# Which sorted edge keys of a segment are counted one by one, and which are first sorted out of a common rest: 76 counting blocks in place of 88

## The reference, cut to what matters

```python
src, dst = edge_index                       # drawn from 0 .. 32767, there are M = 8192 nodes
e     = leaky_relu(a_src[src] + a_dst[dst]) # 4 heads
ee    = exp(e - segment_max(e, dst)[dst])
alpha = ee / (segment_sum(ee, dst)[dst] + 1e-16)
agg   = segment_sum(h[src] * alpha, dst)    # for each node
w     = softmax of the 2 best of 4 scores(layernorm(agg))
out   = x + sum over experts e of w_e * (gelu(x @ W1[e] + b1[e]) @ W2[e] + b2[e])
```

## Time and profile before

| | |
|---|---|
| time, median of 3 runs | 1152.58 us (1148.36 to 1153.88) |
| time of the profiled execution | 1152.78 us |
| its span, first to last instruction | 1151.0 us, so 1.78 us lie around it |
| mean granted clock of TensorE | 0.769 of full speed |
| busy: PE, DVE, ACT, POOL | 802.5, 905.2, 440.0, 611.7 us |

### The profile page before, as it was taken

The page is one execution under the profiler, slowest core; times in us unless marked ns, Lnnn a source line. Parts: engine busy times, 40 slices in busy tenths (PEclk is TensorE's granted clock), DMA queues, the critical chain, the costliest instruction groups (busy, mean ns, idle before and its releaser), DMA issues. The chain is left out here.

```text
span 1151.0 us, 17715 instructions
## 1 busy us (share of the span) xinstructions
PE 802.5 (70%) x5180; PEld 688.4 (60%) x5180; DVE 905.2 (79%) x3070; ACT 440.0 (38%) x1069; POOL 611.7 (53%) x553
## 2 busy tenths in 40 slices
PE   0004888989999988969999999999996415041130
PEld 0003777878888977848888888888884404040030
DVE  7999787867888877997999501888887578989877
ACT  1008788884455544525555553000001212120303
POOL 2000000006777760077777777888887778888004
PEclk9999888888999988979999999555555555555555
DMA  8000011112222112112222300000000012425001
GB/s 251 2 0 28 24 32 43 31 44 48 56 48 63 30 9 27 74 47 65 83 65 83 100 10 9 7 6 7 6 7 9 10 49 82 156 59 178 19 22 37
DMA packets 73043, 55.45 MB, mean 48 GB/s; under 512 B 32534, under 2 KB 65689, under 8 KB 72988
## 3 DMA queue, kind: packets, MB, share of 16 engines
q1 hardware_dynamic: 56140, 48.72, 13.4%
q0 software_dynamic: 16384, 5.54, 5.3%
q10 hardware_dynamic: 464, 0.59, 0.2%
HBM read 36.65 MB, written 17.76 MB: 47 GB/s over the span
## 5 line engine op out<-in xcount | busy, mean ns | idle before, releaser
L554 POOL DMA_INDIRECT sb_arena<-table,sb_arena x384 | 463.7, 1208 | 169.5 <-issue 116.7
L538 POOL DMA_INDIRECT sb_late<-lists,sb_window_at x128 | 127.9, 999 | 297.6 <-DMA lists<-sb_arena 255.9
L729 PE MATMUL ps_four<-sb_late 128*128 128x64 bf16 x1232 | 159.8, 301 | 3.7 <-DVE sb_late L1307 0.3
L1305 DVE TENSOR_TENSOR sb_late<-sb_far_lo,sb_iota_lo 128x1792 bf16<-128x1792 bf16 x88 | 96.1, 1092 | 84.0 <-PE ps_four L729 81.0
L729 PEld LDWEIGHTS ps_four<-sb_late 128*128 128x128 bf16 x1232 | 141.8, 143 | 21.5 <-DVE sb_late L1307 18.3
L702 PE MATMUL ps_four<-sb_we,sb_arena 128*128 128x128 f32 x1024 | 131.9, 282 | 0.0
L702 PEld LDWEIGHTS ps_four<-sb_we,sb_arena 128*128 128x128 f32 x1024 | 119.7, 192 | 14.7 <-issue 14.7
L694 PE MATMUL ps_H<-sb_x2nT,sb_we 128*128 (+1 forms) x512 | 124.7, 388 | 0.0
L887 ACT ACTIVATE sb_arena<-ps_H,sb_be_c 128x256 f32<-128x256 f32 x256 | 107.0, 470 | 30.7 <-PE ps_H L694 28.7
L694 PEld LDWEIGHTS ps_H<-sb_x2nT,sb_we 128*128 128x128 f32 x512 | 95.2, 196 | 11.0
L820 ACT ACTIVATE sb_arena<-sb_arena,sb_owner_mid 128x368 f32<-128x368 f32 x128 | 76.8, 600 | 53.4 <-DVE sb_arena L1048 49.8
(11 more groups left out here) (247 smaller groups left out, 1422.5 us busy)
## 6 DMA issues: line engine op xcount, KB each, us to landing
outputs<-sb_arena SPq DMA_DIRECT2D x24, 512.0 KB, 2.7
sb_arena<-outputs SPq DMA_DIRECT2D x12, 1024.0 KB, 6.3
sb_arena<-in_adj SPq DMA_DIRECT2D x32, 256.0 KB
sb_arena<-table,sb_arena POOLq DMA_INDIRECT x384, 2.8
sb_x2nT<-in_L_ffn_edge_index SPq DMA_DIRECT2D x8, 512.0 KB, 7.6
sb_xs<-in_x SPq DMA_DIRECT2D x32, 128.0 KB, 2.2
out_x<-sb_xs SPq DMA_DIRECT2D x16, 256.0 KB, 2.6
sb_late<-lists,sb_window_at POOLq DMA_INDIRECT x128
```

The costliest lines, as they stand in the source:

```text
L538: pool.indirect_dma_start(bk.bitcast(i32)[:, p * WINDOW:(p + 1) * WINDOW], None, lists, bass.IndirectOffsetOnAxis(ap=window_at[:, p:p + 1] ...
L554: pool.indirect_dma_start(rows[:, g, c, o, :], None, table[0:M, :], bass.IndirectOffsetOnAxis(ap=idxT[:, at:at + 1], axis=0), bounds_check ...
L729: last = nc.tensor.matmul(ps_F, hot_lo[k][:, :, c], hot_hi[k][:, :, c], start=(first and c == 0), stop=(end and c == FB - 1))
L1305: V.tensor_tensor(hot_lo[k], far_lo[:, bass.ds(b * FB, FB)].unsqueeze(1).to_broadcast([P, P, FB]), iota_lo[:, :, :], ALU.is_equal)
```

## The change

Three numbers and the filling of the list are changed. Of each segment the ranks 6 to 35 now stand in the list as they are (30 in place of 36). The ranks 0 to 5 go to `rest`, with the real keys among them set to 0; `rest` grows from 640 to 832 columns, and its 104 largest keys go to the list, by 13 passes in place of 9. The list has 32 x 30 + 104 = 1064 columns, 76 blocks of 14, in place of 1232 columns and 88 blocks. The memset of the 8 spare columns is gone.

```diff
-FULL_FAR, REST_FAR, FARCOLS = 36, 72, 88 * FB
+SKIP_FAR, FULL_FAR, REST_FAR, FARCOLS = 6, 36, 104, 76 * FB
...
-        rest = late[:, LEVCOLS:LEVCOLS + (ECOLS // SEG) * (KEEP1 - FULL_FAR)]
-        far_at = LEVCOLS + (ECOLS // SEG) * (KEEP1 - FULL_FAR)
+        far_at = LEVCOLS + (ECOLS // SEG) * (KEEP1 - FULL_FAR + SKIP_FAR)
+        rest = late[:, LEVCOLS:far_at]
...
-            segments, full_far = ECOLS // SEG, ECOLS // SEG * FULL_FAR
-            V.memset(far_k[:, full_far + REST_FAR:], 0.0)
-            V.tensor_copy(far_k[:, 0:full_far].rearrange("p (g n) -> p g n", g=segments), lev1[:, :, 0:FULL_FAR])
-            plink(V.tensor_copy(rest.rearrange("p (g n) -> p g n", g=segments), lev1[:, :, FULL_FAR:KEEP1]))
+            segments, full_far = ECOLS // SEG, ECOLS // SEG * (FULL_FAR - SKIP_FAR)
+            assert full_far + REST_FAR == FARCOLS
+            V.tensor_copy(far_k[:, 0:full_far].rearrange("p (g n) -> p g n", g=segments), lev1[:, :, SKIP_FAR:FULL_FAR])
+            first_ranks = segments * SKIP_FAR
+            V.scalar_tensor_tensor(rest[:, 0:first_ranks].rearrange("p (g n) -> p g n", g=segments), lev1[:, :, 0:SKIP_FAR], first_real,
+                                   lev1[:, :, 0:SKIP_FAR], ALU.is_lt, ALU.mult)
+            plink(V.tensor_copy(rest[:, first_ranks:].rearrange("p (g n) -> p g n", g=segments), lev1[:, :, FULL_FAR:KEEP1]))
             top([rest], [far_k[:, full_far:full_far + REST_FAR]], REST_FAR // 8)
```

## The result

The changed kernel took 1139.69 us (median of four runs, 1135.1 to 1140.8), the kernel before 1151.72 us on the same chip (1148.36 to 1153.88). The ratio is 0.9898, with a 95% interval of 0.9867 to 0.9929: about 12 us faster. The prediction was 1147.7 us with a range down to 1142.0, so the gain was more than twice the 5.1 us of its sum.

The account below looks back on a forecast made before the run. TensorE was taken to bound the count, VectorE the parts, with gathers 4.2 us from binding part 3. Of 22.3 us saved some 17 became a wait for gathers: 1152.78 - 5.1 = 1147.7 us, range 1142 to 1150.5.

Parts of the forecast that it names:

- Selection: VectorE's sort and list: some 12 us longer, all hidden in its 64.41 us wait for TensorE; cost nothing.
- Twelve blocks fewer: Count stage, paced by TensorE: 12 x 1.855 = 22.3 us less, count ending at 854.2.
- What is late next: GpSimd's gathers ahead of part 3: 12 left at the pair's start, so VectorE waits; some 17 of 22.3 us lost.
- How long the gathers then take: Part 3's pair: one gather held to 9.4 us, the others at 1.30 us; 5.1 us gained in all.
- A gather, once caught, is held until the pair of blocks is over: GpSimd beside VectorE's combine: a caught gather ends about 9.4 us after the pair's beginning.
- n = 2: Two gathers go through in part 3's pair before one is held: scan at 1071.0, 5.1 us gained.
- The term: Loss from a held gather in part 3's pair: 5.1 us gained, against 10.6 us with none held.
- the gathers are not held by the combine: Rival for part 3's pair: 12 gathers take 15.6 us, 10.6 us gained, 1142.2 us; chance 0.10.
- the signs of being wrong: VectorE's wait before the third block vanishing, a block not taking 1.855 us, last gather out outside 1060 to 1068.
- 0.34, 0.10 and 0.03: Chances for faster: n = 3 or more within the likeliest case, gathers not held, VectorE alone setting the end (1130.5).
- the third rival: Gathers behind the held one run at the count's 1.84 us instead of 1.30: 1156.2 us; chance 0.04.
- the first of the twelve would be held: Strict reading of the skill's port rule in part 3's pair, n = 0: 2.5 us gained.

Follow-up runs that it names:

- e6: Kernel before with only the new selection: 13 passes over 832 columns, list padded with zeros to 88 blocks; 1152.26 us, ratio 0.9997.
- e7: Kernel before with its old selection, only the first 76 blocks of its list built and counted, slow path kept off; 1143.34 us, ratio 0.9927.
- e8: Changed kernel with one memset of 64 columns (about 0.1 us) on VectorE ahead of part 3's pair of combined blocks; 1142.3 us, ratio 0.9927.
- e1: Changed kernel with two extra 512 KB loads, meant to run beside part 3's pair but over soon after it began; 1146.02 us, ratio 0.9946.
- e2: Changed kernel with all loads of expert outputs but the first two of twelve cut to 32 bytes a row; 1143.57 us, ratio 0.9934.
- e4: Changed kernel taken further: ranks 8 to 31 as they stand, 184 largest of the rest, 68 blocks, 23 passes over 1024 columns; 1135.55 us, ratio 0.986.
- e3: Changed kernel with VectorE pausing three times in each combined block, each step waiting until the whole step before is done; 1132.5 us, ratio 0.9848.
- e9: Kernel before (88 blocks) with VectorE pausing three times in each combined block; 1156.0 us, ratio 1.0018.
- e10: Changed kernel (76 blocks) with VectorE pausing three times in each combined block, a repeat on the same chip; 1133.34 us, ratio 0.9831.

## Why the prediction was wrong

*Selection: right.* Thirteen passes from 621.81 to 650.20, 2.18 us each, and 52.18 us of wait left where 52 were predicted. e6 shows directly that it costs nothing that can be told.

*Twelve blocks fewer: right.* 22.26 us in the trace against 22.3, at the same pace: (138.5 + 2.6) / 76 = 1.857 us a block by the costliest groups of the profile page (1064 products, as many as 76 blocks have), where the earlier trace rows gave 1.855:

```profile
L729 PE MATMUL ps_four<-sb_late 128*128 128x64 bf16 x1064 | 138.5, 301 | 2.6 <-DVE sb_late L1310 0.2
```

TensorE's granted clock in this stage was again at the 1.2 GHz level, as in the earlier trace rows:

```profile
core 0: us, PE busy (x) PEld busy (x) DVE busy (x) ACT busy (x) POOL busy (x), PEclk, DMA share, GB/s
708.00:847.50 139.50, 136.86 (x1054) 120.97 (x1051) 120.45 (x148) 0.00 (x0) 116.25 (x77) 0.51 0.06 7
```

*What is late next: right in its place.* Part 3 waits for the gathers, 12 of them are left at the pair's start, ScalarE starts 1.72 us after the last one's end (1054.63 - 1052.91) and the scan 3.79 us after that (predicted 1.72 and 3.81). That exactly 12 were left has some luck in it: in the other runs with 76 blocks and no pauses it was 11 (e7), 12 (e8) and 14 (e1, e2).

*How long the gathers then take: this step failed.* "A gather, once caught, is held until the pair of blocks is over" is what the held ones do in pairs without a gap. But the prediction took from it that one must be caught early in every pair, because both pairs of the earlier trace rows had caught one, and chose n = 2. In part 3's pair none was caught in the changed kernel and in e8. In e1, e2, e4 and e7 one was, but at 6.55 us, for 2.82 or 2.83 us: that costs 1.8 us. The term was sized at 5.5 us (10.6 - 5.1), and is 0 to 1.8. The rival "the gathers are not held by the combine", with 10.6 us and a chance of 0.10, came out for this pair: 11.2 by the trace. It is not the rule, as e1, e2, e4 and e7 show. Its time of 1142.2 was 2.5 us too long. 0.6 of that is in the stretch above, 1.1 is the profiled execution of before, which was that much over its median on this chip; the rest is within the spread of the runs. Of the signs of being wrong that the prediction named, the last came: the last gather was out at 1052.91, or 1059.4 with the 6.5 us ahead of the count added, where 1060 to 1068 was allowed. VectorE waited 10.92 us for part 3 in place of some 17.

The chances do not add up as they stand: 0.34, 0.10 and 0.03 make 0.47 for faster, not 0.43, and the third rival, which has 0.04, is counted with 0.05 within 0.5% and with 0.04 as slower.

The evidence to be more careful was in the profile of before. The pairs of the earlier trace rows are those of part 2. Part 1 has two more, which also held gathers (for 5.45 us, and for 4.93 and 3.25 us), so every pair with gathers beside it had caught one, and a hold was the fair guess. But the number that went through first differed (three, none, three, one), and these four stand behind `lowest` or `take_bank`, in the middle of a part, while part 3's pair stands behind the one-hot tiles of `hots_of`. The rule that I drew from them did not say why one gather was caught while three others went through the same instructions, so the case without a hold, or with a late one, deserved more than 0.10.

The Trainium skill (SBUF — State Buffer, section "Who interferes with whom") lets whoever issues first keep the shared ports for the whole instruction. Held gathers agree with it in kind, but an operation of the combine starts every 0.26 us, and a hold of 7.93 us spans some 26 of them. That the first of the twelve would be held, as the prediction took from the section, did not happen: seven went through at 1.00 us each, and the measurement decides. What the section infers of descriptor generation, that tensor_tensor does not stall it, finds no support here: beside the tensor_tensor of the hot blocks 76 gathers started 1.84 us apart, against 1.30 beside the experts. These gathers also read their index tile in SBUF, and no run tells which of the two made them slower.

*What the holds cost elsewhere.* The prediction looked at the holds only in the last pair. The four pairs of parts 1 and 2 hold five gathers of the changed kernel, for 5.46, 3.57, 2.72, 5.45 and 7.93 us. Over 1.00 us each that is 20.1 us, or 15 gathers at 1.30: more than the 12 that were left. This is why e3 removes the whole wait. That it takes the combine's unbroken run to hold a gather is shown by e3, e9 and e10, in which only the pauses differ. It is not enough by itself: part 3's pair in the changed kernel and in e8 has no pause either, and held none. The changed kernel shows once without an edit that a pause ends a hold: in the second pair of part 1 VectorE was idle for 0.04 us behind the 16th operation, 4.28 us into the pair, and the hold ended 0.88 us after that, as the others end 0.87 to 1.01 us after a whole pair:

```profile
948.51 8.61 DVE L1580 SCALAR_TENSOR_TENSOR sb_xs<-sb_arena,sb_gates,sb_xs 128x128 f32<-128x128 f32 x32
```

```profile
950.10 3.57 POOL L554 DMA_INDIRECT sb_arena<-table,sb_arena  x1 [0.30 <-issue]
953.98 1.13 POOL L554 DMA_INDIRECT sb_arena<-table,sb_arena  x1 [0.30 <-issue]
```

## What the runs showed of the hardware

What decides whether a gather of a pair is held was not settled. The offsets, in us after the pair's start, are very regular; these are the pairs that run without a break in the six kernels without pauses and with 68 or 76 blocks (the changed one, e1, e2, e4, e7, e8), one execution each:

| pair | gathers start at | held one starts at, and lasts |
|---|---|---|
| first of part 1 or 2 | -0.02 to 0.00, then every 1.30 | 3.89 to 3.91, 5.45 or 5.46 (10 of 12); 2.58 or 2.59, 6.76 or 6.77 (2) |
| second of part 1 or 2 | 0.20 to 0.25, then every 1.30 | 1.52 to 1.55, 7.93 to 7.95 (9 of 9) |
| ahead of part 3 | 0.05 or 0.06 (e8: -0.02) | 6.55 or 6.56, 2.82 or 2.83 (4 of 6); none (2) |

The combine's operations start every 0.263 us, so five of them take 1.31 us, a little more than a gather and its 0.30 us pause. A gather therefore starts about 0.01 us earlier against the operations than the one before it, and how many go through is, by this reading, how long it takes to drift into some forbidden position. That fits the order of the rows, and it would explain why a few hundredths of a microsecond, or a shift that corrects itself as in e8, can decide over 5 us. It is argued from offsets, not shown. TensorE does not decide it: in e2, where each of the five pairs held one gather, TensorE was busy throughout the first pairs, for 1.4 or 1.5 us of the second ones, and not at all in part 3's.

Shown is what ends it: in e3 VectorE is idle for 0.04 us three times in a block, and the operation ahead of the pause is followed after 0.37 or 0.38 us in place of 0.26 (9.28 us a pair in place of 8.48). A gather of a pair then takes 0.14 us more than 1.00 at most, in place of up to 6.95.

## What to carry to other kernels

When a cut on the bounding engine leaves a second engine late, size the new wait by counting what that engine has left at the point where it is awaited; that count came out here (12, and 11 to 14 in other runs), while the rate at which it would clear them was guessed from two samples. Look also at what holds the second engine earlier: five long rows in the timeline of GpSimd, 20 us together beyond the usual 1.00 us each, were worth more than the wait itself. Making the bounding engine slightly less dense was worth 6 to 8 us here (e3 and e10, by their ratios against the changed kernel's), but only together with the change: on the kernel before, where VectorE did not wait for the gathers, it gained nothing.
